# Third attention: the key blocks of two of its four tiles written by GpSimd instead of VectorE

## What is computed

```python
def _gqa(x, qw, qb, kw, kb, vw, vb, ow, ob):
    q = (x @ qw + qb).reshape(B, S, N_HEADS, HEAD_DIM).transpose(0, 2, 1, 3)
    k = (x @ kw + kb).reshape(B, S, N_KV, HEAD_DIM).transpose(0, 2, 1, 3)
    v = (x @ vw + vb).reshape(B, S, N_KV, HEAD_DIM).transpose(0, 2, 1, 3)
    k = jnp.repeat(k, NUM_REP, axis=1)
    v = jnp.repeat(v, NUM_REP, axis=1)
    scores = jnp.einsum('bhqd,bhkd->bhqk', q, k) / np.sqrt(HEAD_DIM).astype(np.float32)
    attn = jax.nn.softmax(scores, axis=-1)
    out = jnp.einsum('bhqk,bhkd->bhqd', attn, v)
    return out.transpose(0, 2, 1, 3).reshape(B, S, D) @ ow + ob
...
src = x + _gqa(x, qw, qb, kw, kb, vw, vb, ow, ob)
src = _rmsnorm(src, norm1_w)
```

## Time and profile before

| | |
|---|---|
| median of 3 runs | 1545.23 us (1542.59 to 1551.12) |
| profiled execution, its own time | 1543.39 us |
| its span | 1541.6 us |
| PE busy | 1331.8 us (86%) |
| DVE busy | 1098.7 us (71%) |
| ACT busy | 749.6 us (49%) |
| POOL busy | 340.0 us (22%) |
| share of the chain that ended last | PE 57%, DVE 25%, ACT 6%, POOL 2% |
| key blocks (line 460) | 32 on DVE, 38.3 us |

### The profile page before, as it was taken

How to read it: one execution, slowest core, us unless ns; L and a number is a source line. 1 busy time by engine, 2 the same in 40 slices (tenths; PEclk the granted TensorE clock), 3 DMA queues, 4 the chain that set the end, 5 groups by cost and what they waited for, 6 DMA issues and landing times.

```text
span 1541.6 us, 28380 instructions
## 1 busy us (share of the span) xinstructions
PE 1331.8 (86%) x10852; PEld 887.0 (58%) x10852; DVE 1098.7 (71%) x3289; ACT 749.6 (49%) x1422; POOL 340.0 (22%) x282
## 2 busy tenths in 40 slices
PE   4788988897898998888798898889789899888977
PEld 3455744565665664456565575546556567445745
DVE  3556977877666796687775787678776669768774
ACT  0155634674334653575334553467443455357632
POOL 1021210540131130162003032044112123015300
PEclk7799999998999999999999999999999999999999
DMA  9000000000000000000000000000000000000000
GB/s 346 24 1 1 1 1 1 1 1 18 1 7 2 1 1 1 1 1 2 17 1 8 1 1 1 1 1 2 18 1 7 1 1 1 1 0 2 2 1 7
DMA packets 15094, 18.94 MB, mean 12 GB/s; under 512 B 2776, under 2 KB 13672, under 8 KB 14444
## 3 DMA queue, kind: packets, MB, share of 16 engines
q1 hardware_dynamic: 14960, 17.13, 3.3%
HBM read 16.08 MB, written 1.05 MB: 11 GB/s over the span
## 4 chain that ended last, share of the span: by engine, by line
PE 57%; DVE 25%; ACT 6%; issue 6%; POOL 2%; DVEq 0%; POOLq 0%; ACTq 0%
PE bank L1046 7%; PE bank L1057 6%; PE bank L1277 4%; PE bank L1483 4%; PE bank L1488 4%; DVE work L644 3%; DVE small L643 3%; PE bank L854 2%; PE bank L1476 2%; PE bank L1519 2%; DVE small L650 2%; PE bank L502 2%; PE bank L1905 2%; PE bank L1890 2%; PE bank L510 2%
## 5 line engine op out<-in xcount | busy, mean ns | idle before, releaser
L267 POOL TENSOR_TENSOR root<-variance,minus_half 128x2 f32<-128x2 f32 (+1 forms) x72 | 55.2, 767 | 653.0 <-DVE variance L284 405.1
L1099 ACT ACTIVATE work<-bank,w_f 128x512 f32<-128x512 f32 x128 | 87.9, 687 | 88.8 <-PE bank L1046 88.5
L1057 PEld LDWEIGHTS bank<-w_f1d,work 128*128 128x128 f32 x1024 | 119.1, 192 | 13.4 <-issue 13.4
L1057 PE MATMUL bank<-w_f1d,work 128*128 128x129 f32 x1024 | 119.9, 275 | 0.0
L1657 ACT ACTIVATE work<-work,small 128x128 f32<-128x128 f32 x256 | 78.3, 388 | 84.8 <-DVE small L1784 84.8
L1046 PE MATMUL bank<-xnT,w_f 128*128 128x512 f32 x256 | 116.8, 601 | 0.0
L1715 POOL TENSOR_TENSOR small<-small 128x16 f32<-128x16 f32 x32 | 92.9, 2902 | 106.3 <-DVE small L1743 104.6
L643 DVE TENSOR_REDUCE small<-bank 128x8 f32<-128x512 f32 x96 | 65.7, 684 | 30.7 <-PE bank L510 30.5
L1742 DVE TENSOR_REDUCE small<-work 128x16 f32<-128x1024 f32 x48 | 58.4, 1217 | 40.9 <-ACT work L1621 39.3
L1483 PE MATMUL bank<-w_x,cxT 128*128 128x512 f32 x128 | 62.3, 608 | 21.9 <-DVE work L1756 17.1
L1488 PEld LDWEIGHTS bank<-consts,work 128*128 128x128 f32 x576 | 64.2, 140 | 29.2 <-issue 16.8
(11 more groups left out here) (290 smaller groups left out, 3149.7 us busy)
## 6 DMA issues: line engine op xcount, KB each, us to landing
w_f<-in_f_dram SPq DMA_DIRECT2D x1, 2616.0 KB
w_f<-in_f_dram SPq DMA_DIRECT2D x1, 2180.0 KB, 25.3
w_x<-in_x_dram SPq DMA_DIRECT2D x1, 2115.0 KB
w_l<-in_l_dram SPq DMA_DIRECT2D x1, 2088.5 KB, 21.4
w_f1d<-in_f1d_dram SPq DMA_DIRECT2D x4, 512.0 KB
work<-in_x_dram SPq DMA_DIRECT2D x4, 256.0 KB, 3.3
work<-in_ctx_dram SPq DMA_DIRECT2D x4, 256.0 KB, 3.6
out_dram<-x SPq DMA_DIRECT2D x4, 256.0 KB, 2.3
```

The costliest lines, as they stand in the source:

```text
L1057: pe.matmul(z_of(e, t)[:, 0:129], hT[e % 2][:, c, t * P:(t + 1) * P], w_f1d[:, c, e, :], start=(c == 0), stop=(c == 3))
L1099: act.activation(hT[e % 2][:, c, :], banks[n % 3][:, :], ACT.Relu, bias=k_f1["b1"][:, n:n + 1]).then_inc(hT_ready, 1)
```

## The change

In the third attention GpSimd writes the key blocks of tiles 1 and 3 and VectorE those of tiles 0 and 2. GpSimd's part starts with both: it waits for the keys of the first pair and writes the block of tile 1, waits for the keys of the second pair and writes that of tile 3, and then gives the roots as before. Its blocks have a semaphore of their own, `kx_by_pool`, and TensorE waits for it ahead of the scores of tiles 1 and 3. `kx_ready` counts two in a round there. The other two attentions keep their blocks and their counts.

```diff
             def __init__(self, w, src, k_bias, count, key_parts):
...
+                blocks_by_dve = TILES // key_parts
                 self.k_done, self.v_done, self.k_ready, self.v_ready, self.kx_ready = named(
-                    f"k_done:{key_parts} v_done:2 k_ready:{key_parts} v_ready:4 kx_ready:4")
+                    f"k_done:{key_parts} v_done:2 k_ready:{key_parts} v_ready:4 kx_ready:{blocks_by_dve}")
+                self.kx_by_pool, = named("kx_by_pool:2") if key_parts == 2 else (None,)
+
+            def wait_key_block(self, pe, t):
+                if self.kx_by_pool is None:
+                    pe.wait_ge(self.kx_ready, due(self.kx_ready, t + 1))
+                elif t % 2 == 0:
+                    pe.wait_ge(self.kx_ready, due(self.kx_ready, t // 2 + 1))
+                else:
+                    pe.wait_ge(self.kx_by_pool, due(self.kx_by_pool, t // 2 + 1))
...
-            def key_blocks(self, engine, t):
+            def key_blocks(self, engine, t, ready=None):
...
-                                     ALU.mult).then_inc(self.kx_ready, 1)
+                                     ALU.mult).then_inc(ready or self.kx_ready, 1)
...
-                        pe.wait_ge(kv.kx_ready, due(kv.kx_ready, t + 1))
+                        kv.wait_key_block(pe, t)
...
                 @block.gpsimd
                 def _(pool):
+                    if here:
+                        for pair in range(2):
+                            pool.wait_ge(kv.k_ready, due(kv.k_ready, pair + 1))
+                            kv.key_blocks(pool, 2 * pair + 1, kv.kx_by_pool)
                     for pair in range(2):
                         give_root(pool, 2)
...
                         dve.wait_ge(kv.k_ready, due(kv.k_ready, 1))
                         kv.key_blocks(dve, 0)
-                        kv.key_blocks(dve, 1)
...
                             dve.wait_ge(kv.k_ready, due(kv.k_ready, 2))
                             kv.key_blocks(dve, 2)
-                            kv.key_blocks(dve, 3)
```

## The result

The changed kernel takes 1561.91 us (median of 10 runs, 1556.57 to 1568.36) against 1551.26 us for the kernel before in as many runs beside it. The ratio is 1.0071, with a 95% interval of 1.0047 to 1.0096: slower, by some 11 us. All ratios here leave out the few runs of the kernel before that were far slower than the rest, such as one of 2674.02 us among these ten. The forecast was +5.1 us, and 1550 by the median then known, 1545.23; ten runs put that median 6 us higher.

What follows compares the result with a forecast made beforehand. The prediction took VectorE to bound the third attention; +3.3 us from blocked engines and +1.8 from TensorE's clock made +5.1, on the median 1545.23 giving 1550.3, stated as 1550, range 1538 to 1557.

Steps and rivals of the forecast that it cites:

- the collision: Key blocks of the third attention: VectorE and GpSimd exclude each other, whoever comes second waiting for the other's whole instruction.
- bound of 7.7 us: Whole kernel: a measurement tells about 0.5%, 7.7 us, from no change; from +7.7 on it counts as slower.
- First pair: Key blocks of tiles 0 and 1: GpSimd is in first, VectorE's block ends later, +1.45 us in every round.
- Second pair: Key blocks of tiles 2 and 3: +1.38 us in rounds 1 and 4, +0.28 in rounds 2 and 3.
- the race: Which engine starts first at the second pair: GpSimd in rounds 1 and 4, VectorE in rounds 2 and 3.
- TensorE's clock: First scores of the third attention at half clock cost 0.90 us, taken in two rounds of four: +1.8 us.
- My bounds for the clock: Scores in the third attention: from a gain of 2 x 0.63 us to a loss of 4 x 0.90.
- Rival (a): Third attention: VectorE's key block is not held up; 5.8 to 9.3 us gained, put at 1538; chance 17%.
- Rival (b): GpSimd first at every second pair, first scores always half-clocked, +10.6 us, or GpSimd's block over 2.2 us; chance 24%.
- Rival (c): Third attention: nothing moves, since GpSimd's blocks are never waited for and VectorE's losses are hidden; chance 3%.

Runs made afterwards that it cites:

- `after_fill`: The changed kernel with three unused 128x512 matmuls in TensorE's idle time ahead of the third attention's first scores; ratio 1.0018 to the kernel before.
- the second ones: Traces of the kernel before and the changed kernel, both run once more unchanged; ratios 0.9983 and 1.0085 to the kernel before.
- the fills at the end: One unused matmul in each of the third attention's last two idle gaps: changed kernel 1.0011, variant with GpSimd's blocks started after VectorE's 0.9885, against the kernel before.
- `pool_behind`: The changed kernel, but GpSimd starts each block only when VectorE has ended its own of that pair; ratio 0.9951 to the kernel before.

## Why the prediction was right or wrong

**The direction and the collision were right, the clock was not.** Forecast +5.1 us, measured +11, and 1561.9 lies above the range's end of 1557. By the prediction's own bound of 7.7 us this is slower, to which it gave 24%, and not the same, to which it gave 62%. Of the distance to 1550, 6 us are the median of three runs that it was put on. The other 6 are a term that the sum did not have.

**First pair: right.** From the norm's start, the first block ends after 3.56 us in round 1 (368.38 + 1.23 - 366.05) where it ended after 1.97: +1.59; in round 2, 3.44 against 1.96: +1.48. The forecast was +1.45. That the norm itself could be the one held was not foreseen; I had only the other order, GpSimd held by the norm, which is what happened in round 2.

**Second pair: the race was called wrongly in rounds 1 and 4.** I let GpSimd in first there, because the second keys were early in the trace before. VectorE was first in all four. The keys were made at half clock (line 437 takes 1.06 us where 0.59 is usual), so they came last everywhere, VectorE waited for them (0.92 us in round 1), and GpSimd lost by 0.05 us; it was `after_fill` that showed the order I had worked out. I priced the clock and the race as if they were independent, and the clock decides the race.

**TensorE's clock: the failed step.** I put 2 x 0.90 us for first scores at half clock. They took 1.40 us in round 1 and 1.60 in round 3, and 1.09, as is usual, in the other two: 0.8 us, not 1.8. The half clock fell on the second keys and, above all, on the stages behind: outside the attention 11.2 us in the two first traces, 8.4 between the second ones. `after_fill` takes 7.3 to 7.7 of it back and the fills at the end 6.1 to 6.5. My bounds for the clock ended at the stage's own matmuls. I put what the clock costs behind the stage at nothing, without a reason.

**The stage's sum was near by luck.** It is +4.6 us, 107.3 to 111.9, close to the +5.1 that I had for everything. By round it is +0.9, +2.1, +2.2 and -0.5, where the forecast without the clock had +1.38, +0.28, +0.28 and +1.38. Rounds 2 and 3 ran at a granted clock of 0.93 before and 0.88 and 0.87 after, round 4 at 0.88 before and 0.94 after. The errors cancel.

**Rival (a)** is not what this change does, but it is what the change could do: `pool_behind` at 0.9951 is -7.6 us, inside the 5.8 to 9.3 that I gave it. **Rival (b)** named the right amount (+10.6) for wrong reasons: VectorE was first at the second pair in all rounds, and no first scores took 1.99 us. **Rival (c)** fell.

**What stays open.** Which stretches outside run at half clock differs from round to round of one trace (342.5 and 347.9 us for the same instructions in the changed kernel), also far from the attention. That idle time in the stage shifts this pattern, and that matmuls in its gaps take the surplus back, is shown; why the stalled kernels meet the costlier pattern so often, and which gap decides it, is not.

## What to carry to other kernels

Before giving GpSimd a part of VectorE's work, look at what VectorE runs in the same microseconds: here a product with two SBUF inputs waited for the whole of a GpSimd product, and `tensor_scalar` for that or even for zeros being written. So start GpSimd behind them and next to work on PSUM or reductions, as `pool_behind` does. And when a change makes TensorE idle for 3 us where it idled for 1.3, price the clock of what follows, not only the delay; two useless matmuls in gaps were worth 0.6 to 0.7% here, and the work that was moved 0.5%.

## What was not expected of the hardware

A GpSimd product gets in between two back-to-back VectorE instructions: the first norm instruction runs, GpSimd starts, the second waits (2.19 us for a pair of 0.60). GpSimd writing zeros of 128x1024, 0.95 us, holds a `tensor_scalar` but not a two-input product. And four delays of 1.45 us on an otherwise equal kernel cost 1.4% of 1550 us by the ratios, about 21 us, more than three times their own length.
